# A gated cross-attention and binary-weight feed-forward block on one core: attention units moved to other slots of layer one, group parts and weight sums split, high parts moved beside their exponentials

## The reference, cut to what matters

```python
# x: (2, 2048, 512), context: (2, 128, 512), 16 heads of 32, FFN 512 -> 2048 -> 2048 -> 512
h = layernorm(x)
x = x + tanh(g_xattn) * (softmax(Q(h) @ K(ctx).T / sqrt(32)) @ V(ctx)) @ Wo ...
h = layernorm(x)
h = concat([h, -h])                    # 1024 wide
h = relu(s0 * h @ sign(k0)) * 2        # weights are +1 or -1, from booleans
h = relu(s1 * h @ sign(k1)) * 2
x = x + tanh(g_ffn) * s2 * h @ sign(k2)
```

## Time and profile before

| what | value |
|---|---|
| median of 3 runs | 1641.36 us (1639.07 to 1644.02) |
| the profiled execution | 1643.0 us, its span on the core 1641.2 us |
| PE busy | 1523.1 us, 93% of the span |
| DVE busy | 1160.4 us, 71% |
| ACT busy | 762.9 us, 46% |
| POOL busy | 191.0 us, 12% |
| granted clock of PE, mean | 0.988 |

### The profile page before, as it was taken

The page is one execution under the profiler, slowest core; times in us unless marked ns, Lnnn a source line. Parts: engine busy times, 40 slices in busy tenths (PEclk is TensorE's granted clock), DMA queues, the critical chain, the costliest instruction groups (busy, mean ns, idle before and its releaser), DMA issues.

```text
span 1641.2 us, 48157 instructions
## 1 busy us (share of the span) xinstructions
PE 1523.1 (93%) x20568; PEld 1380.2 (84%) x20568; DVE 1160.4 (71%) x2265; ACT 762.9 (46%) x1684; POOL 191.0 (12%) x273
## 2 busy tenths in 40 slices
PE   6799888999999999999999999999999999999999
PEld 4586687988889898888988889897888989888997
DVE  5877678768677776766777676776867777676663
ACT  3442352545545364553545445354554536445341
POOL 2101002010010201102020110201001020110100
PEclk9999999999999999999999999999999999999999
DMA  8442132232433333243332433323242332324200
GB/s 244 111 98 58 42 82 55 70 85 49 89 62 90 62 75 85 50 88 72 72 79 54 91 59 92 66 71 73 52 90 59 90 65 72 76 53 92 35 28 15
DMA packets 283062, 121.09 MB, mean 74 GB/s; under 512 B 249696, under 2 KB 265056, under 8 KB 282848
## 3 DMA queue, kind: packets, MB, share of 16 engines
q1 hardware_dynamic: 280784, 117.48, 32.8%
q10 hardware_dynamic: 2064, 0.53, 0.1%
HBM read 37.76 MB, written 16.78 MB: 33 GB/s over the span
## 4 chain that ended last, share of the span: by engine, by line
PE 56%; DVE 22%; ACT 10%; issue 7%; POOL 3%; DMA 2%; SPq 0%; DVEq 0%; ACTq 0%; POOLq 0%
PE bank L1435 11%; PE bank L1409 10%; PE bank L1410 10%; PE bank L1375 6%; PE bank L1376 6%; ACT Pf L602 4%; DVE nmax L901 3%; DVE h L968 3%; DVE Phl L905 2%; DVE C L941 2%; PE bank L1276 2%; ACT xs L667 2%; PE bank L1277 2%; PE bank L1278 2%; PE bank L1294 2%
## 5 line engine op out<-in xcount | busy, mean ns | idle before, releaser
L1409 PE MATMUL bank<-H,W 128*128 128x128 f16 x6720 | 794.7, 220 | 37.3 <-ACT C L698 34.8
L1410 PE MATMUL bank<-H,W 128*128 128x128 f16 x6720 | 794.1, 220 | 0.0
L1409 PEld LDWEIGHTS bank<-H,W 128*128 128x128 fp8e5 x6720 | 659.8, 99 | 51.1 <-ACT C L698 42.0
L1410 PEld LDWEIGHTS bank<-H,W 128*128 128x128 fp8e5 x6720 | 662.4, 99 | 4.2
L1375 PE MATMUL bank<-hT,W 128*128 128x256 f16 x1024 | 230.0, 274 | 17.7 <-DVE C L941 9.9
L1435 PE MATMUL bank<-W,h 128*128 128x256 fp8e5 x1624 | 208.0, 274 | 28.8 <-DVE h L968 28.3
L1376 PE MATMUL bank<-hT,W 128*128 128x256 f16 x1024 | 229.9, 274 | 0.0
L602 ACT ACTIVATE Pf<-bank,nmax 128x128 f32<-128x128 f32 x496 | 141.9, 369 | 174.4 <-DVE nmax L901 174.4
L549 POOL TENSOR_TENSOR xn<-pvs 128x128 f32<-128x128 f32 x120 | 72.9, 607 | 1083.5 <-DVE pvs L914 1083.5
L1435 PEld LDWEIGHTS bank<-W,h 128*128 128x128 f16 x1624 | 154.3, 98 | 48.0 <-issue 30.3
L941 DVE TENSOR_TENSOR C<-bank,C 128x256 f32<-128x256 f32 x240 | 100.4, 418 | 108.2 <-PE bank L1410 54.5
(11 more groups left out here) (150 smaller groups left out, 2073.3 us busy)
## 6 DMA issues: line engine op xcount, KB each, us to landing
Qst<-q_bounce SPq DMA_DIRECT2D x120, 128.0 KB, 2.8
Y<-in_x_dram SPq DMA_DIRECT2D x16, 512.0 KB, 3.6
R<-X SPq DMA_DIRECT2D x16, 512.0 KB, 3.1
q_bounce<-Qhl SPq DMA_DIRECT2D x120, 64.0 KB
out_dram<-R SPq DMA_DIRECT2D x15, 512.0 KB, 3.3
W<-in_L_ffn_k_dram SPq DMA_DIRECT2D x10, 512.0 KB, 7.3
W<-in_L_ffn_k_dram SPq DMA_DIRECT2D x2, 1024.0 KB, 19.2
PT<-Phl SPq DMA_TRANSPOSE x120, 3.1
```

The lines of the kernel that those rows point to most:

```text
L1409: mm(o, w, H0[:, 0, i, b_of, :], start=first, stop=False, skip_group_check=True)
L1410: last = mm(o, w, H0[:, 1, i, b_of, :], start=False, stop=i == PAIRS - 1, skip_group_check=True)
```

## The change

The tables: the scores of the units stand in slots 11, 14, 17, 19, 21, 23, 25, 27 (before: 14, 17, 19, 21, 23, 25, 27, 29), the weighted sums in 17 to 33 (before 20 to 36), `CT` in 32 and 34, `WO` in 37 and 39 (before 40 and 42), and the first normalisation begins in slot 40 (before 43). Chunk 0 keeps a table of its own (`WEAVE_0`). The high part of a unit's probabilities now follows its exponentials in the same slot on ACT (`EX`); the low part stays in the next slot. The five-row half of `group_hi` is issued in slot P4 for groups 0, 1 and 3, and both halves after the copy of C11 for group 2. The third of the group's sums (`group_last`) and `group_lo` come in P1 and P2 of the next group. The weight sums of chunk 1 are made in quarters. Layer zero uses the three banks in another order.

```diff
-    for u, (scores, values) in enumerate(((14, 20), (17, 22), (19, 24), (21, 26), (23, 28), (25, 31), (27, 33),
-                                          (29, 36))):
...
+        for u, slot in enumerate(scores):
+            put(slot, "S", u)
+            put(slot, "EX", u)
+            put(slot + 1, "PS", u)
+        for u, slot in enumerate(values):
+            put(slot, "PV", u)
...
+    WEAVE = weave((11, 14, 17, 19, 21, 23, 25, 27), (17, 20, 23, 25, 27, 29, 31, 33), (32, 34), 37, 36, 40)
...
+    for slots, q, step, quarters in (((14, 15, 16, 17), 2, 4, range(4)), ((18, 19), 4, 1, (0, 1)),
...
+        for slot, part in zip(slots, quarters):
+            PARTS.setdefault(slot, []).append((q, step, part))
...
-                if kind == "S":
-                    exponents(n, a, bank)
-                if kind == "PS":
+                if kind == "EX":
+                    exponents(n, a, banks[LOOP_BANK["S", n]])
                     act.wait_ge(p_ready, nth(a, NU, n))
...
                     if s == P1:
-                        if n > 0 and not late(f, n - 1):
-                            group_hi(n - 1, f)
                         if late(f, n - 1):
                             act.wait_ge(h1_lo, NH + 1)
                         take(n, s, f, C11)
+                        if n == 3 and not late(f, n - 1):
+                            group_hi(n - 1, f, 0)
+                        if n > 0 and not late(f, n - 1):
+                            group_hi(n - 1, f, 1)
...
                         elif not late(f, n):
-                            act.wait_ge(h2_lo, 2 * group(f, n))
+                            act.wait_ge(h2_lo, 2 * group(f, n) - 1)
                         rectify(n, f, 0, H_R11 + 1, C11[:, :, :])
...
                         rectify(n, f, 2, 0, C12[:, :, :])
+                        if n != 2 and not late(f, n):
+                            group_hi(n, f, 0)
                         act.wait_ge(l1_done, nth(f, NL1, 7 * n + s))
                         rectify(n, f, 3, H_R21 + 1, halves_of(ROLES[n][A]))
...
                     if s == P1 and n > 0 and not late(f, n - 1):
-                        group_lo(n - 1, f)
+                        group_last(n - 1, f)
+                        if n != 3:
+                            group_lo(n - 1, f, 0)
                     if s == P2:
                         dve.wait_ge(l1_copy, copied(f, n, 0))
                         add(n, s, f, C11, banks_of[B])
+                        if n == 3 and not late(f, n - 1):
+                            group_lo(n - 1, f, 0)
+                        if n > 0 and not late(f, n - 1):
+                            group_lo(n - 1, f, 1)
...
-                    if n == 0 and f >= 2:
-                        pe.wait_ge(l1_sum, nth(f - 2, NC, NC - 1))
+                    if n < 2 and f >= 2:
+                        pe.wait_ge(l1_sum, nth(f - 2, NC, NC - 2 + n))
...
-                        o = banks[(n + 1) % 3][:, half * CHUNK:(half + 1) * CHUNK]
+                        o = banks[2 - n % 3][:, half * CHUNK:(half + 1) * CHUNK]
```

More of the change, by code:

```diff
@@ L98, in gated_block_kernel, with weave, put @@
     SLOTS += [("L2", 0, P7), ("L2", 0, P3), ("L1", 2, P4), ("L2", 0, P4)] + [("L1", 3, s) for s in range(7)]
-    WEAVE = {}
-    def weave(slot, kind, n, ahead=1):
-        WEAVE.setdefault(slot, []).append((ahead, (kind, n)))
-    for u, (scores, values) in enumerate(((14, 20), (17, 22), (19, 24), (21, 26), (23, 28), (25, 31), (27, 33),
-                                          (29, 36))):
[L109 to L121, removed]
+    def weave(scores, values, turned, projected, loaded, normalised):
+        where = {}
+        def put(slot, kind, n, ahead=1):
+            where.setdefault(slot, []).append((ahead, (kind, n)))
+        for u, slot in enumerate(scores):
[4 more added lines that the diff above has]
+            put(slot, "PV", u)
+        for t in range(TT):
+            put(turned[t], "CT", t)
+            put(projected + 2 * t, "WO", t)
+            put(projected + 1 + 2 * t, "N2", t)
+            put(projected + 2 + 2 * t, "T2", t)
+        put(loaded, "LOAD", 0)
+        for t in range(TT):
+            put(normalised + t, "LN", t, 2)
+            put(normalised + 2 + t, "N1", t, 2)
+            put(normalised + 3 + t, "T1", t, 2)
+        return where
+    WEAVE_0 = weave((14, 17, 19, 21, 23, 25, 27, 29), (20, 22, 25, 27, 29, 31, 33, 36), (34, 37), 40, 39, 43)
+    WEAVE = weave((11, 14, 17, 19, 21, 23, 25, 27), (17, 20, 23, 25, 27, 29, 31, 33), (32, 34), 37, 36, 40)
     QUERIES, QUERIES_0 = {}, {}
-    for woven_in, made, sent in ((QUERIES, (1, 3, 7, 11), (3, 7, 18, 22)), (QUERIES_0, (5, 9, 12, 14), (9, 12, 18, 22))):
+    for woven_in, made, sent in ((QUERIES, (1, 3, 7, 11), (3, 5, 15, 20)), (QUERIES_0, (5, 9, 12, 14), (9, 12, 18, 22))):
         for g in range(G):
@@ L708, in rectify, with group_hi @@
                         .then_inc(h2_relu if n < 3 else l1_copy, 1)
[L710 to L714, removed]
-                    nc.scalar.activation(h1[:, q % 2, 0, :, rows, :], Fp[:, 1:3, rows.start + 1:rows.stop + 1, :],
-                                         ACT.Copy).then_inc(h2_hi, 1)
+            def group_hi(q, f, n):
+                rows = (EARLY_ROWS, LATE_ROWS)[n]
+                act.wait_ge(h2_step, 3 * group(f, q) + 2 + n)
+                if n == 0:
+                    act.wait_ge(*pass_free(f, q))
+                nc.scalar.activation(h1[:, q % 2, 0, :, rows, :], Fp[:, 1:3, rows.start + 1:rows.stop + 1, :],
+                                     ACT.Copy).then_inc(h2_hi, 1)
             def plain_half(q, half):
@@ L952, in group_sums @@
             def group_sums(q, f):
-                done = 3 * group(f, q)
                 Fg = Fp[:, 1:3]
@@ L1122, in prepare, with weight_step @@
                                                 op1=ALU.bitwise_or).then_inc(w0_made, 1)
-            def weight_step(q, step):
-                Wg, made = (W1[:, q], w1_made[q]) if q < GROUPS else (W2, w2_sums)
-                L11, L12, L21, L22 = (Wg[:, b] for b in range(4))
+            def weight_step(q, step, quarter=None):
+                third = q == GROUPS
+                Wg, made = (W2, w2_sums) if third else (W1[:, q], w1_made[q])
+                parts = range(4) if quarter is None else [quarter]
+                through, pairs = len(parts), slice(2 * parts[0], 2 * parts[-1] + 2)
+                L11, L12, L21, L22 = (Wg[:, b, pairs] for b in range(4))
+                S1, S2, S3, S4 = (Wg[:, b, pairs] for b in (A_S1, A_S2, A_S3, A_S4))
+                ahead = (step - 1) * 4 if not third else 8 * (parts[0] // 2) + 2 * (step - 1)
                 if step == 0:
@@ L1174, in _ @@
                     feed(slot, f)
-                    if f < 2 and s in LATE_WEIGHTS[f]:
-                        weight_step(*LATE_WEIGHTS[f][s])
+                    if f == 0 and s in LATE_WEIGHTS:
+                        weight_step(*LATE_WEIGHTS[s])
+                    if f == 1:
+                        for part in PARTS.get(s, []):
+                            weight_step(*part)
                     if f == 0 and s == 19:
```

81 lines of the change are left out of this document (45 added, 36 removed).

## The result

The changed kernel takes 1733.6 us (median of 4 runs, 1732.6 to 1735.3) against 1642.7 for the kernel before beside it: a ratio of 1.057 (95% interval 1.055 to 1.059). It is slower, by 91 us between the medians and by 89.9 between the spans of the two profiled executions, where 81 were forecast. The profiled execution has a span of 1731.1 us and a mean granted clock of 0.965.

The account below looks back on a forecast made before the run. PE was taken to bound the kernel, so only its pauses and clock count. Terms A to D, +4.2 us a chunk, give +50; with clock and ends +81, forecasting 1722 us, range 1684 to 1750.

Parts of the forecast that it names:

- Term A: Slot 14, pair 7 in P1 of group 0: waits behind unit 0's exponentials and high part; new pause 3.0 us.
- Term B: Pauses at slots 24, 26 and 31: first two shrink by 0.2 and 0.7, third grows 0.4; together -0.5 us.
- Term C: Slots 49 and 0: both waits, 0.45 and 0.9 us, end through later-placed work and bank order; -1.4 us.
- Term D: Slot 47, P7 of group 3: copy of C12 waits on group 2's five-row low part; new pause 3.1 us.
- The disputed price: In Term D, POOL's time for the second projection's scale: 0.9 us taken, pause 3.1; first instruction at 1.35 would give 4.3.
- Term E: The clock, chunks 2 to 13: two falls a chunk at 1.5 us behind the long pauses, +28 us (0 to +50).
- the clock falls no more often: Rival: clock falls only as often as in the kernel before; terms without the clock give 1694 us; chance 0.17.
- Term F: The run's ends: first queries -2.7 us, chunk 14 +4, chunk 1 +4.5, between chunks 0 and 1 -3.
- The other side: Rival: ACT runs ahead of PE through slots 19 to 31, pauses end, new pauses covered; 1561 us, chance 0.06.

## Why the prediction was right

The result lies within the range, and the pauses are where it put them. By its steps:

- **Term A** (pair 7): 3.0 forecast, 3.01 or 3.02 measured in each of chunks 2 to 14. Undone by one order on ACT, made by one number in the kernel before.
- **Term B** (slots 24, 26, 31): -0.5 forecast. Measured 1.2, 0.15 and 2.7 where 1.1 to 1.2, 0.1 and 2.7 were said, together -0.4. From the copy of C22 to that of C11 pass 8.9 us (535.42 to 544.34), forecast 8.8. Of the two causes named for the growth at slot 31, the third sum is worth 0.7 of the pause. The other, a unit's high part ahead of the rectified C12, did not show: with the high parts a slot later the pause grew. The remaining 2.07, which I had carried over from the kernel before without asking, is the place of unit 7's exponentials (with their high part) ahead of the rectified C12. In the kernel before unit 6's exponentials stood in that place; moving them there was not tried.
- **Term C** (slots 49 and 0): -1.4 forecast and measured. I laid slot 49's share to the normalisation leaving slots 45 to 47; with it back in 43 that pause stayed away all the same. What ended it instead was not tried; the parts of the group's sums and low part also moved there.
- **Term D** (P7 of group 3): 3.1 forecast, 3.4 in 9 of 12 chunks and up to 3.8 in the others. The three idle times of DVE were put at 0.5, 0.65 and 1.2 and came as 0.53, 0.71 and 1.22. From the second projection to P7 are 14.1 us in chunk 4 (578.55 to 592.67), not 13.8: DVE's own work came as added up (9.93 us, forecast 9.95), the three idle times are 0.1 longer, and the rest is in gaps of 0.1 us or less between DVE's instructions. The disputed price is settled: POOL's first instruction took 0.19 us (L548, at 580.59) beside DVE's addition from a bank (L1006, at 580.43), where beside the low part it had taken 1.35. That is what the Trainium skill ("SBUF — State Buffer", section on the two separate sides) gives for a DVE instruction with only one input in SBUF.
- **Term E** (clock): +28 forecast, +35 measured. Chunks 2 to 13 last 1256.0 us; 12 periods of 101.0, with the 0.7 by which slot 47 is longer in three of them, are 1213: 43 us, less the 8 of before. The number of falls came as said (24 forecast, 23 found), but two a chunk was a choice and not worked out from rows, so that it fits is in part luck; the price of one was 1.9 and not 1.5 on average, since four lasted twice as long. The prediction also spoke of twelve pauses of 2.3 us in the kernel before: four of the twelve were of 1.7 to 2.1 us, and none of the five falls stood behind those. Filling the pauses gave 41 us back, by another way. The rival "the clock falls no more often" would have been 1694; the run with the pauses filled has no fall at all in chunks 2 to 14 and took 1692.4, so that the rival made real, with the 8 us of falls of before, would be near 1700.
- **Term F** (the ends): -2.7 for the first queries came. Chunk 1 is +5.1 (forecast +4.5) and chunk 0 -6.9 (forecast -3); chunk 14 is +1.9 where +4 was said (the fall counted for it was there before too), and chunk 15 +1.3 where nothing was.

The terms without the clock come to +4.7 a chunk where +4.2 were forecast, so 6 us of the 9 by which the whole is short lie there and 7 in the clock; the ends take 4 back. Part of how close the total comes is thus luck. "The other side" asked for the exchange of ACT and DVE to loosen from slot 14 on; ACT does begin earlier, and the period of that exchange stays at 8.9 us. Yet that rival was right in one thing: the new tables hold a faster kernel. With two placements undone, one pair on DVE exchanged and one unit a slot later, it is 62 us faster than the kernel before, not 91 us slower.

## What to carry to other kernels

On engines that run a written order, an item moved up is paid for by what it is put ahead of: look for the instruction on which the bounding engine's next step hangs, and put nothing with a wait of its own ahead of it. Ask of each old pause too which order makes it, not only whether the change touches it: the two edits that brought the most beyond undoing the new pauses were of that kind (17 and 19 us). A slack of 0.2 us was no cover here, and a pause of the matrix engine costs its own length and, where the clock falls behind it, 1.6 us or more besides.

## What the runs showed of the hardware

- The clock does not go by the length of a single pause. At slot 31, in chunks 2 to 14, it fell behind 2.07 us in none of 13 chunks, and behind 2.2 to 2.3 us in 6 of 9 (the kernel before) and in 3 of 7 (the bank order alone), the shorter ones of those two kernels never; behind 2.75, the only long pause of its chunk, it fell in 4 of 13. In chunks 2 to 13 of the changed kernel it fell behind 3.0 us in 7 of 12, behind 3.4 to 3.8 in 10 of 12, and behind 2.73, with the two others in the same chunk, in 6 of 12. What else decides stays open.
- A pause can be filled with matmuls that nothing needs, and the clock stays at 1.00. The Trainium skill ("TensorE: Matmul & The Clock Gate", section on why this matters for kernels) says that idle gaps between bursts bring the lower level back. These runs agree in kind, though not after each pause: 23 falls followed the 36 long ones. That filling them is worth 41 us in a kernel whose waits it leaves as they are, is this case's own number.
